# Cross-attention in float32 scores by 32-row bands, weighted sums by 32-column bands, and the clamp on GpSimd

## The chip, the cores and the metric

The kernel runs on one core of a Trainium2 chip. The metric is the device time of one execution in microseconds (us), the median of several runs. One execution works through a batch of 64 sequences.

## The reference, cut to what matters

Two blocks follow each other: a cross-attention with 16 heads of 8 columns over 77 keys (what the change rewrites), and a self-attention with a feed-forward part.

```python
# block 0: x (64,128,128), ctx (64,77,128), mask (64,1,128,77), H = 16, hd = 8
q = (query @ Wq + bq).reshape(B, Qlen, H, hd).transpose(0, 2, 1, 3)
k = (key_in @ Wk + bk)...
v = (key_in @ Wv + bv)...
scores = jnp.einsum('bhqd,bhkd->bhqk', q, k) / jnp.sqrt(jnp.float32(hd))
scores = ALPHA * (scores * mask) + (1.0 - ALPHA) * scores      # ALPHA = 0.5
scores = jnp.clip(scores, -50.0, 50.0)
attn = jax.nn.softmax(scores, axis=-1)
context = jnp.einsum('bhqk,bhkd->bhqd', attn, v)
out = context @ Wo + bo
resid = query + out            # then a layer norm with gamma and beta
# block 1: rms norm, q/k/v of 16 heads of 64, rotary, segments of 64 with 16 persistent and
# 16 (equal) memory keys, softmax, to_out_w, residual, rms norm, gated feed-forward of 341
```

## The kernel before

Each engine has its own program, written by hand, and they meet at semaphores. The work of a sequence is cut into three stages: c (cross-attention), a (self-attention up to the weighted values) and f (output projection and feed-forward). `pipeline` (L322) calls each engine's `body(c, a, f)` so that in a pass of the loop stage c works on sequence i+2, a on i+1 and f on i. The order inside `body` is the order in which an engine meets the stages' parts; nothing reorders them. All the parts of a pass thus stand in one fixed queue per engine. PSUM's eight banks are shared out by `banks` (L50): two for stage c, four for a, two for f. The tasks of a stage take its banks in turn, and `cross_free(task)` waits until the task before in that bank was read.

Keys lie on the partitions of the cross scores, so no maximum is taken: the clamp at 50 bounds the exponent. The 16 heads are four groups g of four heads r, and a group's four score maps fill one bank (77 x 512).

- ACT takes q and k from PSUM (L533 to L545): q0T and k0T in float32, q0T_hi and k0T_hi rounded to float32r, then four masked copies of each (qmask_hi keeps the rows of head r of every group, kmask_hi those of group g). POOL works out the rests of the rounding (L418, L419) and spreads them (`lower`, L411 to L414).
- PE `cross_scores(t)` (L840): three float32r matmuls of 512 columns for group t, hi x hi, hi x lo and lo x hi.
- DVE `masked(t)` (L648) multiplies by the mask's weight wT from PSUM into z0, and `clamped(t)` (L653) clamps z0 in place. Their order is masked 0, 1, clamped 0, 1, masked 2, 3, clamped 2, 3. ACT `exp_cross(t)` (L520) follows each clamp.
- PE `weigh_cross(t)` (L848): 16 heads by the exponentials z0. v0's windows are 64 columns wide, 32 of them the values (zero but for the head's own 8), 32 ones that give the sum of the exponentials. Group 2t goes to PSUM partitions 0 to 63, group 2t+1 to 64 to 127.
- DVE `context_sums(t)` (L660) takes the reciprocal of bank pv t, `context(t)` (L664) multiplies two 32-row pieces each into c0T, PE's L996 multiplies by Wo, and DVE goes on with r (L758) and the layer norm.

The rest of the loop that the prediction speaks of: POOL's `rotated(name)` (L406) adds the two halves of the rotary product for q0, k0, q1 and k1, and PE's `turn(name)` (L858, product at L863) waits for it. hn (L702) is the normalised input of the feed-forward. Between PE's turns stand cross scores 2 and 3 and the projection of v1. Behind the turns comes `weigh_cross`, and behind that the products for the self-attention's maxima (L979, L982), which DVE reduces at L730. mt (L735, L739) are the maxima in two bfloat16 parts, PE's shift (L990) turns them, and scores(2), scores(3) (L872) stand between it and L996. A PE row of the profile is one pass of a matmul; a float32 matmul shows two, a float32r or bfloat16 one shows one.

## Time and profile before

| | |
|---|---|
| time, median of 3 runs | 1803.2 us (1799.8, 1803.2, 1804.67) |
| profiled execution | span 1801.7 us from its first to its last instruction, 52360 instructions; its time outside the span is not listed apart, and the three runs' times lie 1.9 below to 3.0 above the span |
| granted TensorE clock | 0.997 of full speed over the span |
| DMA | 26.14 MB, 15 GB/s in the mean |

A row of the timeline gives the start and the length in us, engine, line, operation, what is written and read (partitions x elements), how many instructions were merged, and in brackets the idle time ahead with what ended it. PE's rows hold the latency of a matmul, so rows that follow each other overlap; the distance of the starts is what each takes in a queue. PEld are PE's weight loads.

### The profile page before, as it was taken

The numbers are of one execution on the slowest core, as the hardware profiler recorded it, in microseconds if no ns is written. First come the engines' busy times: TensorE is split into PE (matmuls) and PEld (weight loads), VectorE is DVE, ScalarE is ACT, GpSimd is POOL, SyncE is SP. The second block draws the span as 40 slices with busy tenths as digits, with TensorE's granted clock in tenths as the row PEclk, the third lists the DMA queues.
The fourth block names the chain that finished last, engine by engine and source line by source line (L and its number), as shares of the span: only waits on it lengthen the run. The fifth ranks groups of instructions, "written<-read, shape, count | busy, mean of one in ns | idle before, by whom it ended". The sixth has DMA issues, their size and how long they took to land.

```text
span 1801.7 us, 52360 instructions
## 1 busy us (share of the span) xinstructions
PE 1666.4 (92%) x17891; PEld 1434.9 (80%) x17891; DVE 1543.8 (86%) x3730; ACT 1073.9 (60%) x2637; POOL 856.9 (48%) x1107
## 2 busy tenths in 40 slices
PE   4899999999999999999999999999999999999997
PEld 3788788788888887888888888887888888878876
DVE  5788888889889889888888888888888898898894
ACT  3555656655656656656556556566566556566563
POOL 4344534535535535445445445445355355355352
PEclk9999999999999999999999999999999999999999
DMA  6000000000000000000000000000000000000000
GB/s 176 17 9 11 10 10 11 8 13 11 8 13 11 8 13 11 8 11 12 8 11 13 8 11 13 8 11 8 12 11 8 13 11 8 13 11 8 13 6 6
DMA packets 32411, 26.14 MB, mean 15 GB/s; under 512 B 8118, under 2 KB 31179, under 8 KB 32139
## 3 DMA queue, kind: packets, MB, share of 16 engines
q1 hardware_dynamic: 32394, 25.93, 5.4%
q8 instruction: 9, 0.15, 0.0%
q14 instruction: 8, 0.06, 0.0%
HBM read 21.46 MB, written 4.46 MB: 14 GB/s over the span
## 4 chain that ended last, share of the span: by engine, by line
DVE 49%; PE 22%; issue 21%; ACT 3%; POOL 3%; DVEq 1%; DMA 1%; SPq 0%; ACTq 0%; POOLq 0%
DVE z L658 9%; PE psum L927 6%; DVE ra L641 5%; DVE z L650 5%; DVE rb L644 5%; DVE mx L730 4%; PE psum L854 4%; DVE rden L662 3%; PE psum L898 3%; DVE sT L752 3%; DVE o L676 3%; DVE c0T L668 2%; ACT z L523 2%; POOL st L464 2%; DVE y L770 1%
## 5 line engine op out<-in xcount | busy, mean ns | idle before, releaser
L409 POOL TENSOR_TENSOR ra<-ra,rb 128x512 f32<-128x512 f32 x256 | 332.2, 1324 | 0.2
L464 POOL TENSOR_TENSOR st<-st,nhalf 128x1 f32<-128x1 f32 x64 | 38.3, 598 | 535.4 <-DVE st L763 535.4
L872 PE MATMUL psum<-qpad,kall 128*81 128x128 f32 x2048 | 251.6, 276 | 0.0
L641 DVE TENSOR_TENSOR ra<-psum,rope 128x512 f32<-128x512 f32 x256 | 174.3, 681 | 77.9 <-PE psum L838 77.8
L872 PEld LDWEIGHTS psum<-qpad,kall 128*81 128x81 f32 x2048 | 224.9, 151 | 2.6
L658 DVE TENSOR_SCALAR z<-z 77x512 f32<-77x512 f32 x256 | 216.8, 885 | 0.0
L581 ACT ACTIVATE probs<-psum 81x512 f32<-81x512 f32 x256 | 131.3, 593 | 142.3 <-PE psum L880 142.3
L523 ACT ACTIVATE z<-z 77x512 f32<-77x512 f32 x256 | 154.1, 627 | 67.1 <-DVE z L658 65.5
L854 PE MATMUL psum<-z,v 77*64 77x128 f32 x2048 | 141.6, 280 | 44.9 <-ACT z L523 44.9
L644 DVE TENSOR_TENSOR rb<-psum,rope 128x512 f32<-128x512 f32 x256 | 173.0, 676 | 0.0
L836 PE MATMUL psum<-wqkv_hi,xnT_hi 128*128 128x512 f32 x384 | 168.6, 439 | 2.7 <-DVE xnT_lo L681 1.8
L854 PEld LDWEIGHTS psum<-z,v 77*64 77x64 f32 x2048 | 112.5, 138 | 69.6 <-issue 68.6
L650 DVE TENSOR_TENSOR z<-psum,wT 77x512 f32<-77x512 f32 x256 | 163.1, 674 | 4.8 <-PE psum L846 4.8
L418 POOL TENSOR_TENSOR q0T_rest<-q0T,q0T_hi 128x128 f32<-128x128 f32 x64 | 29.3, 457 | 288.9 <-ACT k0T_hi L537 288.9
L472 ACT ACTIVATE qpad<-psum 64x512 f32<-64x512 f32 x256 | 151.9, 593 | 3.1
L472 ACT ACTIVATE vall<-psum 64x512 f32<-64x512 f32 x256 | 151.2, 591 | 3.1
L838 PE MATMUL psum<-wqkv_hi,xnT_lo 128*128 128x512 f32 x384 | 152.9, 398 | 0.0
L837 PE MATMUL psum<-wqkv_lo,xnT_hi 128*128 128x512 f32 x384 | 152.4, 397 | 0.0
L863 PE MATMUL psum<-cross_w,ra 128*128 128x128 f32 x1024 | 143.2, 273 | 0.1
L863 PEld LDWEIGHTS psum<-cross_w,ra 128*128 128x128 f32 x1024 | 122.2, 141 | 20.7 <-ACT vall L472 0.4
L888 PE MATMUL psum<-vall,probs 81*64 81x65 f32 x4096 | 133.6, 223 | 0.3 <-ACT probs L581 0.3
L888 PEld LDWEIGHTS psum<-vall,probs 81*64 81x64 f32 x4096 | 124.8, 137 | 8.0 <-issue 0.4
(141 smaller groups left out, 4028.3 us busy)
## 6 DMA issues: line engine op xcount, KB each, us to landing
seq_in<-in SPq DMA_DIRECT2D x64, 166.5 KB
out<-out_sb SPq DMA_DIRECT2D x64, 64.0 KB, 1.6
maskT<-in SPq DMA_DIRECT2D x64, 38.5 KB
vall<-memv_dram SPq DMA_DIRECT2D x128, 4.0 KB, 1.9
ctx_all<-in SPq DMA_DIRECT2D x5, 320.0 KB, 12.3
wqkv<-in SPq DMA_DIRECT2D x1, 1536.0 KB, 10.1
stage<-in SPq DMA_DIRECT2D x1, 1296.0 KB
ctx_all<-in SPq DMA_DIRECT2D x3, 288.0 KB, 11.3
```

The costliest lines, as they stand in the source:

```text
L409: nc.gpsimd.tensor_tensor(ra[:, sl], ra[:, sl], rb[:, sl], ALU.add).then_inc(rot_ready, 1)
L472: copy = lambda out, in_, **k: nc.scalar.activation(out, in_, ACT.Copy, **k)
L523: nc.scalar.activation(zt, zt, ACT.Exp, scale=float(HD0) ** -0.5).then_inc(exp0_ready, 1)
L641: V.tensor_tensor(ra[:, sl].rearrange("n (h d) -> n h d", h=8), p, rope[:, 0, :].unsqueeze(1).broadcast_to([S, 8, DH]), ALU.mult)
L644: V.tensor_tensor(rb[:, sl].rearrange("n (h e t) -> n h e t", h=8, t=2), p, rope[:, 1, :].rearrange("n (e t) -> n e t", t=2).unsqueeze(1). ...
L650: V.tensor_tensor(z0[:, 4 * t:4 * t + 4, :], cross_at(f"score{t}")[0:S2, :].rearrange("k (h q) -> k h q", h=4), wT[:].unsqueeze(1).broadca ...
L658: V.tensor_scalar(zt, zt, lim, -lim, ALU.min, ALU.max).then_inc(clip_ready, 1)
L836: mm(self_at(name), xnT_hi[:], wqkv_hi[:, w], stop=False)
L854: last = mm(cross_at(f"pv{t}")[half:half + 64, 0:S], v0_flat[:, lo:lo + 64], z0[:, 4 * g + r, :], start=r == 0, stop=r == 3)
L863: last = nc.tensor.transpose(self_at(f"{name}T")[:, 128 * n:128 * (n + 1)], ra[:, lo + 128 * n:lo + 128 * (n + 1)], ident[:])
L872: mm(self_at(f"score{t}")[0:KEYS, 128 * n:128 * (n + 1)], kall[:, pair, s, :], qpad[:, pair, s, :, :].rearrange("p h i -> p (h i)"), start ...
L888: last = mm(self_at(f"pv{t}")[SEG * s:SEG * (s + 1), VW * n:VW * (n + 1)], probs[:, pair, s, h, :], vall[s][:, w:w + VW])
```

## The change

ACT writes k0T and q0T once each, in float32. POOL spreads k0T alone: kmask[:, r, :] keeps the rows of head r of all four groups. A group's score is now a float32 matmul over its own band of 32 rows (rows 32g to 32g+31 hold its four heads), one matmul per head of 128 columns, two groups taking turns. v0 has windows of 32 columns, and the sums of the exponentials come from products of their own with a table `ones0`; both write bank "pv", columns 0 to 127 and 128 to 255, group g on partitions 32g to 32g+31. One reciprocal and one product of 128 rows make c0T. The clamps move to POOL, between the rotary sums. Stage c has seven PSUM tasks where it had eight. The tiles of the split operands go.

```diff
+VROW = HD0 * GROUP + HD0
...
-                    pool.wait_ge(qk0_ready, c + 1)
-                    nc.gpsimd.tensor_tensor(q0T_rest[:], q0T[:], q0T_hi[:].bitcast(F32), ALU.subtract)
-                    nc.gpsimd.tensor_tensor(k0T_rest[:], k0T[:], k0T_hi[:].bitcast(F32), ALU.subtract).then_inc(rest0_step, 1)
-                    pool.wait_ge(rest0_step, c + 1)
-                    lower(1)
+                def clamped(t):
+                    lim = CLAMP * float(HD0) ** 0.5
+                    zt = z0[:, 4 * t:4 * t + 4, :]
+                    pool.wait_ge(z_ready, c * 4 + (t + 1))
+                    passed(pool, pool_passed)
+                    nc.gpsimd.tensor_scalar(zt, zt, lim, -lim, ALU.min, ALU.max).then_inc(clip_ready, 1)
+
+                if c is not None:
+                    pool.wait_ge(k0_ready, c + 1)
+                    nc.gpsimd.tensor_tensor(kmask[:], headmask.unsqueeze(2).broadcast_to([D, GROUP, S2]),
+                                            k0T[:].unsqueeze(1).broadcast_to([D, GROUP, S2]), ALU.mult).then_inc(kmask_ready, 1)
...
-                if c is not None:
-                    lower(0).then_inc(lo0_ready, 1)
...
-                    for name in QK:
-                        rotated(name)
+                    rotated("q0")
+                    rotated("k0")
+                if c is not None:
+                    clamped(0)
+                    clamped(1)
+                if a is not None:
+                    rotated("q1")
+                    rotated("k1")
+                if c is not None:
+                    clamped(2)
+                    clamped(3)
...
-                    for dst in (q0T, q0T_hi):
-                        nc.scalar.activation(dst[:], p[:, 0:S], ACT.Identity, bias=cols[:, BQ:BQ + 1])
-                    for dst in (k0T, k0T_hi):
-                        last = nc.scalar.activation(dst[:], p[:, S:S + S2], ACT.Identity, bias=cols[:, BK:BK + 1])
-                    last.then_inc(qk0_ready, 1)
-                    for r in range(GROUP):
-                        nc.scalar.activation(qmask_hi[:, r, :], p[:, 0:S], ACT.Identity,
-                                             scale=headmask[:, 0, r:r + 1], bias=head_bias[:, 0, r:r + 1])
-                    for g in range(GROUP):
-                        nc.scalar.activation(kmask_hi[:, g, :], p[:, S:S + S2], ACT.Identity,
-                                             scale=headmask[:, 1, g:g + 1], bias=head_bias[:, 1, g:g + 1])
+                    wait(act, (kmask_ready, c))
+                    nc.scalar.activation(k0T[:], p[:, S:S + S2], ACT.Identity, bias=cols[:, BK:BK + 1]).then_inc(k0_ready, 1)
+                    nc.scalar.activation(q0T[:], p[:, 0:S], ACT.Identity, bias=cols[:, BQ:BQ + 1])
...
-                def context_sums(t):
-                    wait(dve, cross_filled(f"pv{t}", c))
-                    V.reciprocal(rden0[:, t, :], cross_at(f"pv{t}")[:, 0:S]).then_inc(cross_step, 1)
+                def context_sums():
+                    wait(dve, cross_filled("pv", c))
+                    V.reciprocal(rden0[:], cross_at("pv")[:, S:2 * S]).then_inc(cross_step, 1)
+
+                def context():
+                    wait(dve, (cross_step, cross_steps[1]("rden0", c)))
+                    V.tensor_tensor(c0T[:], cross_at("pv")[:, 0:S], rden0[:], ALU.mult).then_inc(c0T_ready, 1)
...
-                    masked(0)
-                    masked(1)
-                    clamped(0)
-                    clamped(1)
-                    masked(2)
-                    masked(3)
-                    clamped(2)
-                    clamped(3)
+                    for t in range(4):
+                        masked(t)
...
-                def cross_scores(t):
-                    wait(pe, cross_free(f"score{t}", c))
-                    out = cross_at(f"score{t}")[0:S2, :]
-                    q_hi, q_lo = (m[:].rearrange("p r i -> p (r i)") for m in (qmask_hi, qmask_lo))
-                    mm(out, kmask_hi[:, t, :], q_hi, stop=False)
-                    mm(out, kmask_hi[:, t, :], q_lo, start=False, stop=False)
-                    mm(out, kmask_lo[:, t, :], q_hi, start=False).then_inc(cross_fill(f"score{t}"), 1)
+                def cross_scores(*groups):
+                    for g in groups:
+                        wait(pe, cross_free(f"score{g}", c))
+                    for r in range(GROUP):
+                        for g in groups:
+                            rows = slice(32 * g, 32 * (g + 1))
+                            last = mm(cross_at(f"score{g}")[0:S2, S * r:S * (r + 1)], kmask[rows, r, :], q0T[rows, :], start=r == 0)
+                            if r == GROUP - 1:
+                                last.then_inc(cross_fill(f"score{g}"), 1)
+
+                def weigh_cross(*groups):
+                    for r in range(GROUP):
+                        window = slice(32 * r, 32 * (r + 1))
+                        for g in groups:
+                            mm(cross_at("pv")[32 * g:32 * (g + 1), 0:S], v0[:, g, window], z0[:, 4 * g + r, :], start=r == 0)
+                        for g in groups:
+                            last = mm(cross_at("pv")[32 * g:32 * (g + 1), S:2 * S], ones0[:, window], z0[:, 4 * g + r, :], start=False)
+                    return last
...
+                    wait(pe, cross_free("pv", c))
+                    pe.wait_ge(exp0_ready, c * 4 + 2)
+                    weigh_cross(0, 1)
+                    pe.wait_ge(exp0_ready, c * 4 + 4)
+                    weigh_cross(2, 3).then_inc(cross_fill("pv"), 1)
```

How the queues move. On POOL, in the loop, the stretch from the pow of the feed-forward's norm (st) to the copy of memk; `ra` is the rotary sum, `z` the clamp. Before:

```order
L424 TENSOR_TENSOR st<-st,nhalf 128x1
L413 TENSOR_TENSOR qmask_lo<-cross_w,q0T_rest 128x512
L407 ISA
L409 TENSOR_TENSOR ra<-ra,rb 128x512
L407 REGISTER_ALU
L409 TENSOR_TENSOR ra<-ra,rb 128x512
L407 REGISTER_ALU
L409 TENSOR_TENSOR ra<-ra,rb 128x512
L407 REGISTER_ALU
L409 TENSOR_TENSOR ra<-ra,rb 128x512
```

And now:

```order
L420 TENSOR_TENSOR st<-st,nhalf 128x1
L403 ISA
L405 TENSOR_TENSOR ra<-ra,rb 128x512
L403 REGISTER_ALU
L405 TENSOR_TENSOR ra<-ra,rb 128x512
L410 ISA
L412 TENSOR_SCALAR z<-z 77x512
L410 REGISTER_ALU
L412 TENSOR_SCALAR z<-z 77x512
L403 REGISTER_ALU
L405 TENSOR_TENSOR ra<-ra,rb 128x512
```

Two clamps stand ahead of q1's and k1's rotary sums, and two more behind k1's.

On DVE, in the loop, from the last rotary product (rb of k1) to the first copy of kall. Before:

```order
L644 TENSOR_TENSOR rb<-psum,rope 128x512
L709 REGISTER_ALU
L99 ISA
L650 TENSOR_TENSOR z<-psum,wT 77x512
L99 REGISTER_ALU
L650 TENSOR_TENSOR z<-psum,wT 77x512
L658 TENSOR_SCALAR z<-z 77x512 x2
L650 TENSOR_TENSOR z<-psum,wT 77x512
L99 REGISTER_ALU
L650 TENSOR_TENSOR z<-psum,wT 77x512
L658 TENSOR_SCALAR z<-z 77x512
```

And now:

```order
L638 TENSOR_TENSOR rb<-psum,rope 128x512
L692 REGISTER_ALU
L100 ISA
L644 TENSOR_TENSOR z<-psum,wT 77x512
L100 ISA
L644 TENSOR_TENSOR z<-psum,wT 77x512
L100 REGISTER_ALU
L644 TENSOR_TENSOR z<-psum,wT 77x512
L100 REGISTER_ALU
L644 TENSOR_TENSOR z<-psum,wT 77x512
L100 ISA
L700 COPY kall<-psum 128x8x64
```

The four masks stand together, each behind a wait of its own.

On PE, in the loop, from the last turn (k1) to the first product for the maxima; `z` and `v` are the weighted sums. Before:

```order
L863 MATMUL psum<-cross_w,ra 128x128 x4
L99 REGISTER_ALU
L854 MATMUL psum<-z,v 64x128 x8
L99 REGISTER_ALU
L854 MATMUL psum<-z,v 64x128 x8
L972 REGISTER_ALU
L979 MATMUL psum<-causal_b,ident_b 128x4x64
```

And now, where the first four rows of sums come four times for groups 0 and 1 and as often for groups 2 and 3:

```order
L836 MATMUL psum<-cross_w,ra 128x128 x4
L100 REGISTER_ALU
L826 MATMUL psum<-z,v 32x128 x2
L828 MATMUL psum<-z,ones 32x128 x2
L826 MATMUL psum<-z,v 32x128 x2
L828 MATMUL psum<-z,ones 32x128 x2
```

16 matmuls of 64 weight columns have become 32 of 32 columns, in the same place.

## Rows read from the trace of the kernel before

**Rows 1.** The page, busy time of each engine, and the chain by engine

```profile
PE 1666.4 (92%) x17891; PEld 1434.9 (80%) x17891; DVE 1543.8 (86%) x3730; ACT 1073.9 (60%) x2637; POOL 856.9 (48%) x1107
...
DVE 49%; PE 22%; issue 21%; ACT 3%; POOL 3%; DVEq 1%; DMA 1%; SPq 0%; ACTq 0%; POOLq 0%
```

**Rows 2.** The chain in order of time: start us, us, what

```profile
917.72 0.32 PE psum L905
...
944.97 0.32 PE psum L905
```

**Rows 3.** Timeline of DVE, 923.4 to 941.5

```profile
924.04 0.60 DVE L702 TENSOR_SCALAR hn<-x,st 128x128 f32<-128x128 f32 x1
...
926.96 1.27 DVE L650 TENSOR_TENSOR z<-psum,wT 77x512 f32<-77x512 f32 x2
928.15 1.85 DVE L658 TENSOR_SCALAR z<-z 77x512 f32<-77x512 f32 x2
929.93 1.27 DVE L650 TENSOR_TENSOR z<-psum,wT 77x512 f32<-77x512 f32 x2
931.13 1.56 DVE L658 TENSOR_SCALAR z<-z 77x512 f32<-77x512 f32 x2
...
935.11 1.72 DVE L730 TENSOR_REDUCE mx<-psum 128x4 f32<-128x324 f32 x4 [0.36 <-PE psum L982]
...
938.62 1.19 DVE L668 TENSOR_TENSOR c0T<-psum,rden 32x128 f32<-32x128 f32 x4
...
940.63 0.28 DVE L758 TENSOR_TENSOR r<-psum,xb 128x128 f32<-128x128 f32 x1
```

**Rows 4.** Timeline of POOL, 923.4 to 934.9

```profile
923.00 0.55 POOL L424 TENSOR_TENSOR st<-st,nhalf 128x1 f32<-128x1 f32 x1 [0.23 <-DVE st L692]
923.52 1.03 POOL L413 TENSOR_TENSOR qmask_lo<-cross_w,q0T_rest 128x512 fp32r<-128x512 f32 x1
924.52 5.20 POOL L409 TENSOR_TENSOR ra<-ra,rb 128x512 f32<-128x512 f32 x4
...
932.97 0.29 POOL L457 TENSOR_SCALAR y_keep<-y 128x128 f32<-128x128 f32 x1
```

**Rows 5.** Timeline of PE, 924 to 941.5

```profile
925.01 0.42 PE L844 MATMUL psum<-qmask_hi,kmask_hi 128*77 128x512 f32 x1
...
931.17 0.60 PE L863 MATMUL psum<-cross_w,ra 128*128 128x128 f32 x4
931.70 1.09 PE L854 MATMUL psum<-z,v 77*64 77x128 f32 x16
933.49 1.09 PE L854 MATMUL psum<-z,v 77*64 77x128 f32 x16 [0.69 <-ACT z L523]
934.62 0.28 PE L979 MATMUL psum<-causal_b,ident_b 128*128 128x256 bf16 x1
...
938.00 0.22 PE L990 MATMUL psum<-stack_b,mt 128*64 128x64 bf16 x1
938.15 1.97 PE L872 MATMUL psum<-qpad,kall 128*81 128x128 f32 x16
939.96 0.39 PE L996 MATMUL psum<-cross_w,c0T 128*128 128x128 f32 x2
```

**Rows 6.** Timeline of ACT, 929 to 936

```profile
932.72 0.63 ACT L523 ACTIVATE z<-z 77x512 f32<-77x512 f32 x1 [0.52 <-DVE z L658]
```

**Rows 7.** Timeline of DVE in the first sequence, 21 to 31, POOL idle

```profile
24.76 0.75 DVE L658 TENSOR_SCALAR z<-z 77x512 f32<-77x512 f32 x2
```

**Rows 8.** Groups by line of POOL, 0 to 60: busy us, mean ns | idle

```profile
L452 POOL TENSOR_TENSOR wqkv_lo<-wqkv,wqkv_hi 128x3072 fp32r<-128x3072 f32 x1 | 6.7, 6695 | 4.1 <-ACT wqkv_hi L472 4.1
```

**Rows 9.** Timelines of PE, first sequence and 915; a group of weight loads

```profile
24.38 1.98 PE L854 MATMUL psum<-z,v 77*64 77x128 f32 x16 [0.26 <-ACT z L523]
...
915.05 2.09 PE L888 MATMUL psum<-vall,probs 81*64 81x65 f32 x64
...
L872 PEld LDWEIGHTS psum<-qpad,kall 128*81 128x81 f32 x2048 | 224.9, 151 | 2.6
```

More of the change, by code:

```diff
@@ L158, in build @@
         k0T = sb("k0T", [D, S2])
-        q0T_hi, k0T_hi = sb("q0T_hi", [D, S], F32R), sb("k0T_hi", [D, S2], F32R)
-        q0T_rest, k0T_rest = sb("q0T_rest", [D, S]), sb("k0T_rest", [D, S2])
-        qmask_hi, qmask_lo = (sb(n, [D, GROUP, S], F32R) for n in ("qmask_hi", "qmask_lo"))
-        kmask_hi, kmask_lo = (sb(n, [D, GROUP, S2], F32R) for n in ("kmask_hi", "kmask_lo"))
-        VB = 4 * HD0 + 40
-        v0 = sb("v0", [S2, 4, 4, VB])
+        kmask = sb("kmask", [D, GROUP, S2])
+        v0 = sb("v0", [S2, GROUP, GROUP * VROW])
+        ones0 = sb("ones0", [S2, GROUP * VROW])
         z0 = sb("z0", [S2, H, S])
-        rden0 = sb("rden0", [128, 2, S])
+        rden0 = sb("rden0", [128, S])
         c0T = sb("c0T", [D, S])
@@ L596, in _ @@
             dve.wait_ge(cross_w_in, CROSS_WEIGHTS_IN)
-            for which, bias in ((0, BQ), (1, BK)):
-                V.tensor_scalar(head_bias[:, which, :], headmask[:, which, :], cols[:, bias:bias + 1], None, ALU.mult)
             dve.wait_ge(setup_pe, 1)
@@ L651, in masked @@
                                     wT[:].unsqueeze(1).broadcast_to([S2, 4, S]), ALU.mult).then_inc(z_ready, 1)
-                def clamped(t):
-                    lim = CLAMP * float(HD0) ** 0.5
-                    zt = z0[:, 4 * t:4 * t + 4, :]
-                    dve.wait_ge(z_ready, c * 4 + (t + 1))
-                    passed(dve, dve_passed)
-                    V.tensor_scalar(zt, zt, lim, -lim, ALU.min, ALU.max).then_inc(clip_ready, 1)
-                def context_sums(t):
-                    wait(dve, cross_filled(f"pv{t}", c))
-                    V.reciprocal(rden0[:, t, :], cross_at(f"pv{t}")[:, 0:S]).then_inc(cross_step, 1)
-                def context(t):
-                    wait(dve, (cross_step, cross_steps[1](f"rden{t}", c)))
-                    for half in (0, 64):
-                        row = 64 * t + half // 2
-                        last = V.tensor_tensor(c0T[row:row + 32, :], cross_at(f"pv{t}")[half:half + 32, 0:S],
-                                               rden0[half + 32:half + 64, t, :], ALU.mult)
-                    last.then_inc(c0T_ready, 1)
+                def context_sums():
[4 more added lines that the diff above has]
+                    V.tensor_tensor(c0T[:], cross_at("pv")[:, 0:S], rden0[:], ALU.mult).then_inc(c0T_ready, 1)
                 def normalised(t):
@@ L724, in body @@
                                       self_at(f"k{t}T").rearrange("p (c s j) -> p c s j", c=4, s=NSEG)).then_inc(k_ready, 1)
-                if c is not None:
-                    context_sums(0)
                 if a is not None:
@@ L742, in body @@
                 if c is not None:
-                    context_sums(1)
-                if c is not None:
-                    context(0)
-                    context(1)
+                    context_sums()
+                    context()
                 if f is not None:
@@ L838, in project @@
                     mm(self_at(name), xnT_lo[:], wqkv_hi[:, w], start=False).then_inc(self_fill(name), 1)
-                def cross_scores(t):
-                    wait(pe, cross_free(f"score{t}", c))
-                    out = cross_at(f"score{t}")[0:S2, :]
-                    q_hi, q_lo = (m[:].rearrange("p r i -> p (r i)") for m in (qmask_hi, qmask_lo))
-                    mm(out, kmask_hi[:, t, :], q_hi, stop=False)
-                    mm(out, kmask_hi[:, t, :], q_lo, start=False, stop=False)
-                    mm(out, kmask_lo[:, t, :], q_hi, start=False).then_inc(cross_fill(f"score{t}"), 1)
-                def weigh_cross(t):
-                    wait(pe, cross_free(f"pv{t}", c))
-                    pe.wait_ge(exp0_ready, c * 4 + (2 * t + 2))
-                    for r in range(4):
-                        for g in (2 * t, 2 * t + 1):
-                            half, lo = 64 * (g % 2), 4 * VB * g + 64 * r
-                            last = mm(cross_at(f"pv{t}")[half:half + 64, 0:S], v0_flat[:, lo:lo + 64],
-                                      z0[:, 4 * g + r, :], start=r == 0, stop=r == 3)
-                    last.then_inc(cross_fill(f"pv{t}"), 1)
+                def cross_scores(*groups):
[15 more added lines that the diff above has]
+                    return last
                 def turn(name):
@@ L941, in body @@
                     pe.wait_ge(qkv0_ready, c + 1)
-                    pe.wait_ge(lo0_ready, c + 1)
-                    cross_scores(0)
-                    cross_scores(1)
+                    pe.wait_ge(kmask_ready, c + 1)
+                    cross_scores(0, 1)
                 if f is not None:
```

39 lines of the change are left out of this document (15 added, 24 removed).

## The prediction

> **What bounds the kernel now.** The page comes first [rows 1]: DVE is busy 86% of the span, PE 92% (modelled ends), POOL 48%, and the chain that ended last runs 49% on DVE and 22% on PE. So the loop is a ring of hand-overs and not one full engine. The chain in order of time shows the ring's length: xnT's transpose (L905) starts at 917.72 and again at 944.97 [rows 2], 27.25 us for one sequence. All times below are of this one pass. DVE's timeline [rows 3] shows the work around the change: the masks z (L650) from 926.96, two at a time, the clamps (L658), the maxima (L730) from 935.11, four small c0T products (L668), r (L758) at 940.63. PE's timeline [rows 5] gives what those wait for: scores 0 (L844) from 925.01, the last turn of k1 (L863) at 931.17, weighted sums (L854) at 931.70 and 933.49, the first maxima product (L979) at 934.62, shift (L990) at 938.00, the last scores (L872) up to L996 (wo) at 939.96. POOL [rows 4] adds ra and rb four times, 5.20 us, 1.30 each, from 924.52 to 929.72, ahead of need.
>
> **The change part by part.**
>
> *ACT* loses ten activations and writes k0T first; it waits for others in this stretch, so I cost that at nothing. Its cover is PE's three projections before L844. POOL's kmask product replaces four products, the last of which (L413) ends at 924.55 [rows 4]. POOL then starts its first ra+rb right behind the pow (L424), at 923.55 and not at 924.52.
>
> *hn.* hn (L702) took 0.60 us and ended at 924.64, 0.09 after POOL's L413 ended at 924.55 [rows 3, 4]: it stood behind a POOL operation. The first ra+rb now covers it and ends at 924.85, so hn ends near 924.94: DVE +0.30. The masks then start at 927.26.
>
> *Clamps, price on POOL.* No POOL clamp is in the trace. DVE's took 0.75 us for two with POOL idle [rows 7], 1.85 and 1.56 beside POOL [rows 3]; 0.37 each is my lower end. The nearest POOL row is y_keep's tensor_scalar with two constants, 128 columns in 0.29 [rows 4]. A POOL operation with two inputs costs 1.30 for 512 columns and 6.70 for 3072 [rows 4, 8], 2.1 ns a column and some 0.2 fixed. With the same 0.2 fixed, y_keep's 0.29 leaves 0.7 to 0.9 ns a column, so 512 columns cost 0.2 + 0.45 = 0.65. I take 0.65, since that row is the same operation. Upper ends: 1.03, the product with a repeated input (L413), and 1.30.
> The Trainium skill ("GPSIMD Engine Reference", section Key points) speaks against the move: for elementwise work DVE is about twice as fast. No POOL clamp here can confirm it. An estimate by it is 0.75 for a clamp (twice 0.37), and the forecast at the end would be about 1890.
>
> *Clamps, place on POOL.* The order is q0, k0, clamp 0, clamp 1, q1, k1, clamp 2, clamp 3. k0 ends at 924.9 + 1.3 = 926.2. Mask 0 ends near 927.95 (0.635 a mask, two in 1.27 [rows 3]), so POOL now stands idle from 926.2 to 928.0 with q1 and k1 queued behind that wait. Then clamps 0 and 1 to 929.3, q1 and k1 to 931.9 (were 929.72), clamps 2 and 3 to 933.2, exp 3 (0.63 [rows 6]) to 933.9.
>
> *DVE.* 3.41 us of clamps leave it (1.85 + 1.56), but this does not bring the later masks forward: masks 2 and 3 need scores that PE starts only when masks 0 and 1 have emptied both banks (928.55), so they run near 929.95, as before. DVE idles instead.
>
> *Scores on PE.* Twelve records with 512 moving columns become 32 with 128. A float32 record of this length with full rows takes 0.109 (16 in 1.97, less the 0.27 tail), and 0.054 where two column halves take turns (16 in 1.09) [rows 5]. Two 32-row bands take turns here, which no row shows. Ends: 0.054 and 0.109, 0.9 or 1.75 us for two groups. I take 0.054. It costs nothing either way: the first two groups start at 925.3 (925.01 plus hn's 0.3), and at 0.109 they are full at 925.3 + 1.75 + 0.27 = 927.3, as DVE comes free for them (927.26), and masks 2 and 3 end at 932.65, before POOL is at clamp 3.
>
> *Weighted sums on PE.* 32 records become 64, since the sums of weights are products of their own. Each call has 32 records over two column bands: at 0.054 that is 1.74 per call where 0.9 stood. L888 gets 0.03 a record, but with 65 moving columns [rows 9]: per column it is the same rate, so fewer weight columns should buy nothing. Upper end 0.109, if bands of 32 did not run side by side.
>
> *Sum up to the maxima.* k1 turned: 931.9 + 0.1, 0.45 of issue, to 932.45. Groups 0 and 1 from 932.5 to 934.25, groups 2 and 3 (exp 3 is done at 933.9) to 936.0. L979 starts at 936.05 instead of 934.62: **+1.43**.
>
> *After the maxima.* DVE: one reciprocal is left; the first stood in an idle gap before the maxima, worth nothing. c0T falls from 1.19 to about 0.29 (one product of 128 rows, as r's [rows 3]): -0.9. PE: shift at 938.00 + 1.43 = 939.43, eight scores behind it, wo at 939.96 + 1.43 = 941.39. PE was just in step with c0T; now it is the later one, so most of the 0.9 is lost. wo is full 0.44 later (as 939.96 to 940.40) at 941.83, and r, at 940.63 before, starts there: **+1.20** per sequence. From r to the next L905 DVE works as before (ending at 944.97), and its sums (L888) come 1.43 later on PE, just in time.
>
> *Total.* 63 passes hold both parts: 63 x 1.20 = 76. The first sequence has nothing to hide its longer sums, and the clock is at its lower level there (16 records in 1.98 [rows 9] against 1.09): about +2. The profiled span is 1801.7, the median 1.5 above: 1801.7 + 76 + 2 + 1.5 = **1881**.
>
> **Bounds.** Clamp 0.37: clamp 1 ends 928.9, k1 931.5, L979 935.6, +0.75 a pass: 1852. Clamp 1.03: k1 ends 932.7, clamp 3 934.7, exp 3 935.4, L979 937.25, +2.4: 1956. At 1.30: L979 938.3, 2025.
>
> **Rivals.**
> *A, faster.* DVE's relief decides. For it: 49% of the chain is DVE, and the clamps cost double beside POOL. It needs a clamp of 0.37 and sums at 0.027 a record. Then k1 ends at 931.5, L979 starts at 934.0, 0.62 earlier, and with a wo no longer late (-0.23) a pass is 0.85 shorter: 1801.7 - 54 + 2 + 1.5 = 1751. It turns where L979 starts before 934.85. Against it: the columns' rate of L854 and L888, and POOL's idle wait. 6%.
> *B, slower by the row bands.* Their weight loads (0.15 each, L872 on PEld [rows 9]) are not hidden. At 0.109 + 0.15 a record scores 0 and 1 fill only at 929.7, scores 2 and 3 at 936.1, and L979 starts near 940.5: +5.6, 2160. From about 0.12 on it begins to cost; half-way (0.17) L979 is at 937.95, +3.1 a pass, 2000. Against it: L854's loads hide in the same kind of turn. 7%.
> *C, clamp as a two-input operation,* 1.03 to 1.30: 1956 to 2025. Against it: y_keep. 6%.
> *D, no relief and no harm:* the 0.3 of hn does not come and the waits pack tighter than my 0.1 a hand-over, with a clamp of 0.37: within 0.3%, up to 1809. 3%.
> *E, the bands of 32 columns do not overlap:* 3.5 us per call, L979 at 939.5, +4.7 a pass: 2101. 2%.
>
> **Numbers.** Forecast 1881, its cases from 1835 (the 0.37 clamp and 0.25 us fewer in hand-overs) to 1956: 76%. A measurement of this kernel tells 0.3% (5 us) from nothing. Faster 6%, same 3%, slower 91% (forecast, B, C and E). The range 1835 to 1970 holds the forecast's cases and the near end of C, the larger part of its 6%; A, B, D, E and the rest, 2 in 10, lie outside.
>
> **What would show it.** After: L905 to L905 near 28.45; POOL's clamps 0.6 to 0.7 each, with idle time of some 1.8 before clamp 0, released by DVE's mask; DVE busy share down to about 65%; 32 sum records in about 2.0 us; L979 right behind the last sum with no wait for exp 3; r waiting for L996. It is wrong if q1 and k1 end before 931, if a clamp is above 0.8 (then exp 3 releases the last sums), if score records are above 0.12, or if DVE still has no idle time ahead of masks 2 and 3.

## The result, and the profile after

| | before | after |
|---|---|---|
| time, median (lowest to highest) | 1801.85 us (1799.80 to 1804.67) | 1820.99 us (1819.94 to 1823.03) |
| span of the profiled execution | 1801.7 us | 1821.2 us |
| one pass (xnT's transpose to the next) | 27.25 us | 27.53 us |
| granted TensorE clock | 0.997 | 0.996 |

The ratio is 1.0102, with a 95% interval of 1.0087 to 1.0118. The change makes the kernel slower, by 19 us where the prediction said 78 and put its lower end at 1835.

First the page of the changed kernel: busy time of each engine, the chain by engine, and two groups (line, engine, operation; busy us, mean ns; idle time ahead and who ended it).

```profile
PE 1707.5 (94%) x21219; PEld 1511.1 (83%) x21219; DVE 1232.4 (68%) x3216; ACT 874.1 (48%) x1997; POOL 840.0 (46%) x1172
...
PE 38%; issue 31%; DVE 16%; POOL 13%; POOLq 1%; DMA 1%; DVEq 0%; SPq 0%; ACT 0%; ACTq 0%
...
L705 DVE TENSOR_REDUCE mx<-psum 128x4 f32<-128x324 f32 x256 | 109.0, 487 | 183.7 <-PE psum L956 183.7
L412 POOL TENSOR_SCALAR z<-z 77x512 f32<-77x512 f32 x256 | 153.3, 614 | 148.5 <-DVE z L644 148.5
```

Against [rows 1], DVE went from 86% to 68% busy and from 49% to 16% of the chain, and the time still rose. POOL, 3% of the chain before, now holds 13%, and waits 148.5 us for masks. DVE waits 183.7 us for the maxima products. The relief of DVE turned into waiting.

POOL's timeline of one pass, which begins at 927.42 (start, length, line; the bracket is the idle time ahead and its end):

```profile
932.47 0.55 POOL L420 TENSOR_TENSOR st<-st,nhalf 128x1 f32<-128x1 f32 x1 [1.58 <-DVE st L675]
932.99 2.52 POOL L405 TENSOR_TENSOR ra<-ra,rb 128x512 f32<-128x512 f32 x2
937.55 1.20 POOL L412 TENSOR_SCALAR z<-z 77x512 f32<-77x512 f32 x2 [2.05 <-DVE z L644]
938.72 2.52 POOL L405 TENSOR_TENSOR ra<-ra,rb 128x512 f32<-128x512 f32 x2
```

A clamp takes 0.60 on POOL. Ahead of clamp 0 POOL is idle for 2.05 us with q1 and k1 queued behind it; k1 is added at 941.24, 13.82 us into the pass, where it was 12.0 before (929.72 in [rows 4]).

PE's timeline of the same pass:

```profile
934.84 1.10 PE L818 MATMUL psum<-q0T,kmask 32*77 32x128 f32 x16
...
940.13 0.63 PE L836 MATMUL psum<-cross_w,ra 128*128 128x128 f32 x4 [0.77 <-POOL ra L405]
...
941.94 0.41 PE L826 MATMUL psum<-z,v 77*32 77x128 f32 x4
942.18 0.39 PE L828 MATMUL psum<-z,ones 77*32 77x128 f32 x4
...
943.27 0.43 PE L826 MATMUL psum<-z,v 77*32 77x128 f32 x8
943.49 0.43 PE L828 MATMUL psum<-z,ones 77*32 77x128 f32 x8
943.75 0.39 PE L826 MATMUL psum<-z,v 77*32 77x128 f32 x4
...
945.16 0.28 PE L953 MATMUL psum<-causal_b,ident_b 128*128 128x256 bf16 x1
...
950.19 0.39 PE L970 MATMUL psum<-cross_w,c0T 128*128 128x128 f32 x2
```

L953 is the old L979, L970 the old L996. PE now waits 0.77 for the first turn that follows the clamps. The 64 records of the sums take 3.22 us from 941.94 to 945.16. Four records take 0.22; but at 943.27 and 943.49, where the first call (groups 0 and 1) meets the second (2 and 3), eight records pass in 0.22 and the next eight in 0.26.

DVE's timeline of the same pass:

```profile
932.09 0.29 DVE L675 CUSTOM_DVE_ANT_0 x1sq<-x 128x128 f32<-128x128 f32 x1
...
933.67 0.70 DVE L685 TENSOR_SCALAR hn<-x,st 128x128 f32<-128x128 f32 x1
...
936.68 1.27 DVE L644 TENSOR_TENSOR z<-psum,wT 77x512 f32<-77x512 f32 x2
939.40 1.28 DVE L644 TENSOR_TENSOR z<-psum,wT 77x512 f32<-77x512 f32 x2 [1.44 <-PE psum L818]
...
945.64 1.70 DVE L705 TENSOR_REDUCE mx<-psum 128x4 f32<-128x324 f32 x4 [2.90 <-PE psum L956]
...
949.14 0.29 DVE L653 TENSOR_TENSOR c0T<-psum,rden 128x128 f32<-128x128 f32 x1
...
950.62 0.29 DVE L731 TENSOR_TENSOR r<-psum,xb 128x128 f32<-128x128 f32 x1 [0.41 <-PE psum L970]
```

The idle time stands where the prediction put it: 1.44 ahead of masks 2 and 3, and r waits 0.41 for wo.

The same stretch as positions in the pass, worked out from these rows and those of before:

| us into the pass | before | predicted | after |
|---|---|---|---|
| masks start | 9.24 | 9.54 | 9.26 |
| k1 added on POOL | 12.00 | 14.18 | 13.82 |
| first weighted sum | 13.98 | 14.78 | 14.52 |
| first maxima product | 16.90 | 18.33 | 17.74 |
| wo (L996, L970) | 22.24 | 23.67 | 22.77 |
| r | 22.91 | 24.11 | 23.20 |

The spans differ by 19.5, and it adds up like this. The first xnT product starts at 35.31 in both kernels. The second starts at 73.64 where it was 70.64: 3.0 in one sequence. There too POOL meets clamp 0 ahead of q1 and k1, and waits 9.45 us for its mask (the first row below): k1's rotary sum ends at 58.52 where it ended at 48.00, and the weighted sums start 2.13 later, at 60.58 against 58.45. The clock was lower for a part of it. The third is at 101.19 (97.88), the last at 1780.88 (1762.33): 18.55 less 3.31 is 15.2 over 61 passes, 0.25 each, since seven passes before were longer than 27.25 (27.52 to 28.48). The end after the last adds 0.95. After the change, a row of POOL's timeline, two of PE's, and the windows row of 58 to 62 (PE, PEld, DVE, ACT, POOL busy, then the granted clock):

```profile
54.85 1.21 POOL L412 TENSOR_SCALAR z<-z 77x512 f32<-77x512 f32 x2 [9.45 <-DVE z L644]
```

```profile
35.31 0.45 PE L878 MATMUL psum<-cross_w,xn 128*128 128x128 f32 x1 [3.74 <-DVE xn L758]
73.64 0.33 PE L878 MATMUL psum<-cross_w,xn 128*128 128x128 f32 x1 [0.65 <-DVE o L659]
```

```profile
58.00:62.00 4.00, 4.00 (x34) 3.24 (x34) 1.32 (x3) 2.81 (x5) 2.49 (x6) 0.64 0.17 35
```

### The profile page after: what moved, and what is told of

Same layout as the page of the kernel before. It is cut to its first block, busy times and chain, and to the rows that moved or that the text cites. A ratio compares the mean times of both kernels' runs of the same rounds, so it can differ in the third digit from the quotient of the medians.

```text
span 1821.2 us, 57993 instructions
## 1 busy us (share of the span) xinstructions
PE 1707.5 (94%) x21219; PEld 1511.1 (83%) x21219; DVE 1232.4 (68%) x3216; ACT 874.1 (48%) x1997; POOL 840.0 (46%) x1172
## 4 chain that ended last, share of the span: by engine, by line
PE 38%; issue 31%; DVE 16%; POOL 13%; POOLq 1%; DMA 1%; DVEq 0%; SPq 0%; ACT 0%; ACTq 0%
PE psum L845 13%; PE psum L826 6%; PE psum L828 5%; POOL ra L405 5%; DVE rb L638 4%; DVE ra L635 4%; PE psum L836 4%; POOL kmask L416 2%; DVE z L644 2%; PE psum L956 2%; POOL st L467 2%; POOL z L412 2%; POOL st L420 2%; PE psum L953 2%; DVE bn L733 1%
## 5 line engine op out<-in xcount | busy, mean ns | idle before, releaser
L405 POOL TENSOR_TENSOR ra<-ra,rb 128x512 f32<-128x512 f32 x256 | 322.2, 1280 | 0.1
L845 PE MATMUL psum<-qpad,kall 128*81 128x128 f32 x2048 | 251.8, 276 | 0.0
L705 DVE TENSOR_REDUCE mx<-psum 128x4 f32<-128x324 f32 x256 | 109.0, 487 | 183.7 <-PE psum L956 183.7
L845 PEld LDWEIGHTS psum<-qpad,kall 128*81 128x81 f32 x2048 | 225.0, 151 | 2.7
L412 POOL TENSOR_SCALAR z<-z 77x512 f32<-77x512 f32 x256 | 153.3, 614 | 148.5 <-DVE z L644 148.5
L836 PE MATMUL psum<-cross_w,ra 128*128 128x128 f32 x1024 | 147.6, 277 | 48.9 <-POOL ra L405 48.3
L836 PEld LDWEIGHTS psum<-cross_w,ra 128*128 128x128 f32 x1024 | 112.3, 141 | 82.5 <-issue 81.4
L826 PE MATMUL psum<-z,v 77*32 77x128 f32 x2048 | 179.7, 278 | 0.7 <-DVE z L644 0.7
L828 PE MATMUL psum<-z,ones 77*32 77x128 f32 x2048 | 178.0, 275 | 0.0
L416 POOL TENSOR_TENSOR kmask<-cross_w,k0T 128x308 f32<-128x308 f32 x64 | 45.2, 707 | 242.7 <-ACT k0T L538 242.7
L475 ACT ACTIVATE hnT<-psum,cols 128x128 f32<-128x128 f32 x64 | 23.6, 368 | 277.7 <-PE psum L912 277.7
L818 PE MATMUL psum<-q0T,kmask 32*77 32x128 f32 x2048 | 142.7, 277 | 11.7 <-DVE z L644 8.8
```

Source lines behind the costliest of these rows:

```text
L405: nc.gpsimd.tensor_tensor(ra[:, sl], ra[:, sl], rb[:, sl], ALU.add).then_inc(rot_ready, 1)
L412: nc.gpsimd.tensor_scalar(zt, zt, lim, -lim, ALU.min, ALU.max).then_inc(clip_ready, 1)
L475: copy = lambda out, in_, **k: nc.scalar.activation(out, in_, ACT.Copy, **k)
L826: mm(cross_at("pv")[32 * g:32 * (g + 1), 0:S], v0[:, g, window], z0[:, 4 * g + r, :], start=r == 0)
L828: last = mm(cross_at("pv")[32 * g:32 * (g + 1), S:2 * S], ones0[:, window], z0[:, 4 * g + r, :], start=False)
L836: last = nc.tensor.transpose(self_at(f"{name}T")[:, 128 * n:128 * (n + 1)], ra[:, lo + 128 * n:lo + 128 * (n + 1)], ident[:])
```

## The experiments

The theory: the loss comes from where the clamps stand in POOL's queue and from the longer sums, and neither a cheaper DVE nor the new scores cost anything. The rivals: the move to GpSimd itself is what hurts, or the new scores are; or the bands of 32 columns do not share the array. Each run is named by its change against the kernel before or after, and a ratio is to the kernel before as it was run beside it, with its 95% interval. The probes e3, e6 and e8 stand below with their times.

| run | scores | sums | clamps | time us | ratio |
|---|---|---|---|---|---|
| before | old | old | DVE | 1801.9 | 1 |
| after | new | new | POOL, between | 1821.0 | 1.010 |
| e1 | new | new | POOL, behind | 1764.5 | 0.980 (0.977 to 0.984) |
| e2 | new | new | DVE | 1763.7 | 0.979 (0.976 to 0.981) |
| e4 | new | new, one call | POOL, between | 1810.0 | 1.004 (1.003 to 1.006) |
| e5 | old | old | POOL, between | 1801.1 | 1.000 (0.999 to 1.001) |
| e7 | new | old | POOL, between | 1802.6 | 1.001 (0.999 to 1.002) |
| e9 | new | new, one call | POOL, behind | 1758.2 | 0.976 (0.974 to 0.977) |
| e10 | new | new, one call | DVE | 1771.9 | 0.982 (0.980 to 0.984) |
| e11 | new | old | DVE | 1753.6 | 0.974 (0.972 to 0.976) |
| e12 | new | old | POOL, behind | 1745.8 | 0.968 (0.967 to 0.969) |

### e1_late_clamps: the clamps behind all four rotary sums

```diff
-                    rotated("q0")
-                    rotated("k0")
+                    for name in QK:
+                        rotated(name)
                 if c is not None:
-                    clamped(0)
-                    clamped(1)
-                if a is not None:
-                    rotated("q1")
-                    rotated("k1")
-                if c is not None:
-                    clamped(2)
-                    clamped(3)
+                    for t in range(4):
+                        clamped(t)
```

> The changed kernel with POOL's order q0, k0, q1, k1, then clamps 0 to 3. Theory 1 (POOL's queue order is the costly part: q1 and k1 stand behind a wait for DVE's mask, 2.05 us idle per pass in the changed trace): k1's rotary sum ends about 3 us earlier, the sums start behind k1's turn near 13.4 us into a pass instead of 14.5, L953 starts near 16.7 instead of 17.7, and the pass falls by 0.9 to 1.0: about 1760 (1745 to 1775), faster than both kernels. Theory 2 (PE's longer sums alone make the kernel slower, what POOL does is hidden): within 4 us of 1821.

Measured 1764.54 us (1763.37 to 1771.19), ratio 0.9803. POOL's timeline of this run, one pass, and then the chain by engine:

```profile
903.77 3.91 POOL L405 TENSOR_TENSOR ra<-ra,rb 128x512 f32<-128x512 f32 x3
907.65 1.18 POOL L412 TENSOR_SCALAR z<-z 77x512 f32<-77x512 f32 x2
909.84 1.21 POOL L412 TENSOR_SCALAR z<-z 77x512 f32<-77x512 f32 x2 [1.00 <-DVE z L638]
```

```profile
PE 80%; DVE 10%; issue 5%; POOL 3%; DMA 1%; DVEq 0%; ACT 0%; SPq 0%; ACTq 0%; POOLq 0%
```

The 2.05 us of idle time ahead of clamp 0 are gone, and the idle time that is left, ahead of clamp 2, holds up no rotary sum. The move of the clamps behind the rotary sums is worth 56 us, and the chain now runs 80% on PE. The place in the queue is the cause, not the engine.

### e2_dve_clamps: the clamps back on DVE, in the old order

```diff
-                    for t in range(4):
-                        masked(t)
+                    masked(0)
+                    masked(1)
+                    clamped(0)
+                    clamped(1)
+                    masked(2)
+                    masked(3)
+                    clamped(2)
+                    clamped(3)
```

> The changed kernel with the clamps back on DVE in the old order (masks 0, 1, clamps 0, 1, masks 2, 3, clamps 2, 3), bands and sums as changed. Theory 1: k1 is turned early again, but exp 3 comes as late as before the change (about 15.9 us into a pass), so groups 2 and 3 of the sums end near 17.5, and the time lies between the two kernels, 1810 (1802 to 1818). Rival (the clamp on POOL is in itself what costs, since it is slower there than a free DVE): below 1795.

Measured 1763.71 us (1762.89 to 1764.33): 46 us below the expectation. By its number this is the rival's result (below 1795), but not by its cause: e1 leaves the clamps on POOL and takes 1764.5. Two clamps on DVE took 0.91 and 1.00 here, where [rows 3] has 1.85 and 1.56. DVE's timeline, then POOL's:

```profile
907.72 0.91 DVE L636 TENSOR_SCALAR z<-z 77x512 f32<-77x512 f32 x2
...
910.48 1.00 DVE L636 TENSOR_SCALAR z<-z 77x512 f32<-77x512 f32 x2
```

```profile
902.83 5.16 POOL L405 TENSOR_TENSOR ra<-ra,rb 128x512 f32<-128x512 f32 x4
907.94 0.41 POOL L426 COPY kall<-memk 128x16 f32 x1
...
910.53 0.67 POOL L436 TENSOR_TENSOR xb<-seq_in,rows 128x128 f32<-128x128 f32 x1
```

POOL's timeline of before, beside clamps 2 and 3:

```profile
931.11 1.29 POOL L445 TENSOR_TENSOR ug<-ug,half_gate 128x384 f32<-128x384 f32 x1
```

Without the split operands POOL starts its rotary sums earlier and ends them at 907.99, 0.27 us into the first two clamps. In the kernel before, clamps 0 and 1 lay almost wholly beside the rotary sums (928.15 to 930.00 against an end at 929.72) and took 1.85. In all four cases the second clamp of a pair ends 0.28 or 0.29 behind the end of a POOL operation beside it: 930.00 behind 929.72 and 932.69 behind 932.40 before, 908.63 behind 908.35 and 911.48 behind 911.20 here. That the price follows the POOL operation beside it is my reading of these rows; no run moved the overlap alone.

### e3_no_weight_sums: the sums of the exponentials left out

```diff
-                        for g in groups:
-                            last = mm(cross_at("pv")[32 * g:32 * (g + 1), S:2 * S], ones0[:, window], z0[:, 4 * g + r, :], start=False)
```

> The changed kernel without the products with ones0, so without the sums of the exponentials: it divides by the weighted values instead, and its output is not the attention's. 64 records fall to 32. Theory 1: L953 then starts behind exp 3, near 16.65 us into a pass (was 17.74), ACT's value copy holds the fourth maxima product again as before the change, and the time is 1788 (1780 to 1796), 33 below the changed kernel. If PE's sums were hidden: within 4 us of 1821.

Measured 1787.10 us (1785.71 to 1792.27). The reciprocal is taken of the weighted values instead, so the result is no attention; the work is otherwise the same. PE's timeline, the fourth maxima product:

```profile
926.41 0.28 PE L951 MATMUL psum<-causal_b,ident_b 128*128 128x256 bf16 x1 [0.24 <-ACT vall L475]
```

Half the records gone give 34 us, and a wait caps it: with the sums early, the fourth maxima product waits for ACT's copy of values(1) (vall). This wait is a step that the prediction did not have.

### e4_four_bands: all four groups in one call behind exp 3

```diff
-                    pe.wait_ge(exp0_ready, c * 4 + 2)
-                    weigh_cross(0, 1)
...
-                    weigh_cross(2, 3).then_inc(cross_fill("pv"), 1)
+                    weigh_cross(0, 1, 2, 3).then_inc(cross_fill("pv"), 1)
```

> The changed kernel with all four groups taking turns in one call of the weighted sums, which then waits for exp 3 (15.6 us into a pass, the sums began at 14.5). If bands of 32 columns run side by side however many they are (at the joint of the two calls 16 records passed in 0.48 us, where four took 0.22 each time elsewhere): 0.027 us a record, the sums end near 17.5, 1803 (1795 to 1812). If only two can: 0.055 a record, they end near 19.2, 1910 (1890 to 1925).

Measured 1809.98 us (1808.93 to 1814.83): 11 us faster than after, 7 above the expected 1803 and within its 1795 to 1812. PE's timeline:

```profile
912.30 0.42 PE L826 MATMUL psum<-z,v 77*32 77x128 f32 x8 [1.10 <-ACT z L526]
912.54 0.40 PE L828 MATMUL psum<-z,ones 77*32 77x128 f32 x8
912.76 0.40 PE L826 MATMUL psum<-z,v 77*32 77x128 f32 x8
...
914.18 0.28 PE L951 MATMUL psum<-causal_b,ident_b 128*128 128x256 bf16 x1
```

Eight records per 0.22 us throughout: four bands of 32 columns run side by side, 0.027 a record where two bands give 0.055. The 64 records take 1.88 instead of 3.22. This confirms what the joint of the two calls showed.

### e5_before_pool_clamps: the kernel before, with only the clamps moved

The edit is that of the change's own diff for `clamped`, in the kernel before.

> The kernel before with only the clamps moved: POOL's order q0, k0, clamps 0 and 1, q1, k1, clamps 2 and 3, masks 0 to 3 in a row on DVE; operands, scores and sums stay. By the schedule: clamps of 0.60, k1's rotary sum ends 13.8 us into a pass instead of 12.0, exp 3 at 15.7 as before, ACT's value copy still holds the fourth maxima product (18.1), so the move alone costs nothing: 1802 (1794 to 1808). Rival (the clamps' place costs the 40 us by which the two variants of the changed kernel with other places were faster): above 1820.

Measured 1801.06 us (1799.84 to 1807.20), ratio 1.0000. In the kernel before, the move buys and costs nothing. Its fourth maxima product shows the wait again:

```profile
932.63 0.28 PE L982 MATMUL psum<-causal_b,ident_b 128*128 128x256 bf16 x1 [0.23 <-ACT vall L488]
```

### e6_before_sums_twice: the kernel before, half of its sums run twice

```diff
-                    for r in range(4):
+                    for r in (*range(4 * t), *range(4)):
```

> The kernel before with the weighted sums of groups 2 and 3 run twice (the second run starts the accumulation again, so the output is the same): L979 comes about 0.87 us later, as late in a pass (17.75) as in the changed kernel. If the old tail on DVE (maxima, mt, reciprocal, four c0T products, sT, r, end to end) has no slack, a pass grows by nearly all of it: 1850 (1842 to 1858). If such a delay is absorbed there as in the changed kernel (0.28 of 0.84): 1820.

Measured 1849.72 us (1846.93 to 1852.47). Sixteen more records (0.87 us) cost 0.75 a pass. So in the kernel before almost nothing catches longer sums, since r stands there at the end of DVE's serial part: what longer sums cost in the changed kernel depends on its shorter DVE part.

### e7_old_sums and e8_four_products: what the new sums cost and give

e7 puts the old sums into the changed kernel (windows of 64 columns, 32 records, two banks, two reciprocals, four products). e8 keeps the new sums, but makes c0T by four products of 32 rows:

```diff
-                    V.tensor_tensor(c0T[:], cross_at("pv")[:, 0:S], rden0[:], ALU.mult).then_inc(c0T_ready, 1)
+                    for row in range(0, 128, 32):
+                        last = V.tensor_tensor(c0T[row:row + 32, :], cross_at("pv")[row:row + 32, 0:S],
+                                               rden0[row:row + 32, :], ALU.mult)
+                    last.then_inc(c0T_ready, 1)
```

> The changed kernel with the old weighted sums (64-column windows with their ones, 32 records, two banks, two reciprocals, four c0T products); clamps on POOL, bands for the scores. L953 starts behind exp 3 at 16.65 us into a pass, ACT's value copy holds the fourth product, DVE's tail is as before: as the kernel before, 1803 (1796 to 1810). If the longer sums were not what moved the time (POOL's queue alone): within 4 us of 1821.

> The changed kernel with c0T by four products of 32 rows (1.2 us on DVE where one took 0.29). In its trace c0T was ready 0.76 before PE came to L970 and r waited 0.41 for L970. So of the 0.9 more 0.45 should show per pass: 1849 (1842 to 1857), which is the size of what the one product had given. If PE alone sets r: 1821.

Measured: e7 1802.64 us (1800.87 to 1807.88), e8 1856.76 (1853.17 to 1858.50). The new sums cost 18 us as they stand, and without the shorter c0T they would cost 54. e7 differs from e5 by the scores alone, 1802.6 against 1801.1: as long as POOL's queue holds the clamps between the rotary sums, the new scores are worth nothing.

### e9_late_four, e10_dve_four, e11_dve_old_sums: combinations

e9 is e1 with e4's single call, e10 is e2 with it, and e11 is e2 with e7's old sums, so that of the change only the scores are left.

> The changed kernel with both orders altered: POOL adds q0, k0, q1, k1 before the four clamps, and the weighted sums of all four groups run in one call behind exp 3, each record over its own band of 32 columns. With the late clamps alone exp 3 ended at 911.71 and the maxima products followed the last sum at about 913.8. In one call 64 records took 1.76 us (912.30 to 914.06 in the run with four bands alone), so here 911.75 to 913.5: up to 0.3 us a pass earlier, until the fourth maxima product waits for ACT's copy of values(1), which ends at 914.16 there. My theory: PE is now the bound and waits stand behind it, 1752 to 1764, likeliest 1758. Rival, that the sums of groups 0 and 1 filled an idle stretch ahead of exp 3 which now stays empty: 1768 or more.

> The changed kernel with the clamps back on DVE in the old order, and the sums of all four groups in one call behind exp 3. With the clamps on DVE alone exp 3 ended at 912.14 and the sums ran from 910.90 to 914.1; here 912.2 to 913.96, some 0.12 to 0.15 earlier: 1750 to 1763, likeliest 1756. Rival: the exps, now the last to be waited for, move with DVE beside POOL, and the sums start later than 912.5: 1770 or more.

> The changed kernel with the clamps back on DVE and the old sums with windows of 64 columns (32 records, two banks, two reciprocals, four products): of the change only the float32 scores in 32-row bands are left. The sums end about 1 us earlier than with 64 records, but the fourth maxima product then waits for ACT's copy of values(1) (which ended at 914.59 with the clamps alone), and DVE has the serial tail of four products again, with r at about 919.6, as in the run with the clamps alone. My theory: 1757 to 1770, likeliest 1764, so that the new scores alone give all of the gain. Rival: the serial tail of DVE costs again what it cost before (0.9 us a pass), 1790 or more.

e9: 1758.22 us (1754.36 to 1759.97), at its expected 1758. e11: 1753.55 us (1751.33 to 1759.35), 10 us below the likeliest 1764 and below the range. Its steady pass is 26.47 against 26.66 in e2: the serial tail on DVE gives r at 22.13 into the pass, where I had taken e2's 22.32. The tail of four products is longer than e2's (5.52 from the maxima to r against 4.97), but the maxima start 0.74 earlier, 16.61 into the pass against 17.35.

e10: 1771.88 us (1766.85 to 1779.61), above its range and above the rival's 1770, but not for the rival's reason alone. Its steady pass is 26.61, 0.05 shorter than e2's, which would give a span of about 1759; the profiled one is 1777.7. Here the clock decides. Busy time of the engines by stretch (PE, PEld, DVE, ACT, POOL, then the granted clock), and PE's timeline there:

```profile
221.00:222.50 1.50, 1.33 (x48) 1.33 (x52) 0.66 (x2) 1.44 (x4) 0.04 (x1) 1.00 0.49 140
222.50:224.00 1.50, 1.50 (x35) 1.22 (x28) 0.31 (x1) 1.05 (x2) 0.00 (x0) 0.73 0.00 0
224.00:225.50 1.50, 1.50 (x16) 1.37 (x14) 1.50 (x4) 0.00 (x0) 0.00 (x0) 0.50 0.00 0
225.50:227.00 1.50, 1.50 (x11) 1.50 (x10) 1.37 (x6) 0.00 (x0) 0.00 (x0) 0.63 0.00 0
```

```profile
221.17 0.43 PE L823 MATMUL psum<-z,v 77*32 77x128 f32 x8 [1.23 <-ACT z L510]
...
227.61 0.22 PE L959 MATMUL psum<-stack_b,mt 128*64 128x64 bf16 x1
...
921.76 0.43 PE L823 MATMUL psum<-z,v 77*32 77x128 f32 x8 [1.24 <-ACT z L510]
```

After 1.23 us idle and 1.9 us of sums the granted clock fell to 0.50, the level of 1.2 GHz, for some 3.4 us, and came back while PE was busy throughout. From the first maxima product (223.06) to the shift this pass took 4.55 us; another pass of the same run took 3.10 (923.65 to 926.75), although PE had been idle as long ahead of its sums, 1.24 us. Twelve passes of this trace took 28.04 to 28.09 instead of 26.61, 17.4 us together. e9 has the same call behind an idle stretch of 1.11 us, and its trace shows a clock of 1.00 from 200 to 1700. The kernel before has one such stretch, from 142 to 146, in a pass of 28.48. Why the clock falls in one pass and not in the next, these runs don't tell.

### e12_late_old_sums: the fastest

The changed kernel with e1's order of POOL and e7's old sums.

> The changed kernel with the clamps on GpSimd but behind all four rotary sums (q0, k0, q1, k1, then clamps 0 to 3), and the old sums with windows of 64 columns, two reciprocals and four products. Compared with the run that has the clamps on DVE and the old sums (1753.6, a pass of 26.47): there the second half of the sums waited 0.30 for exp 3 and the fourth maxima product 0.22 for ACT's copy of values(1), which stands behind exp 3 on ACT. Into a pass, exp 3 ends 0.19 earlier with the late clamps on GpSimd (14.77 against 14.96) and that copy about 0.13 earlier (17.22 against 17.35); the serial tail on DVE is the same. My theory: 0.05 to 0.13 a pass, so 1745 to 1751, likeliest 1748. Rival: the tail on DVE binds and not ACT's copy, so that nothing is gained: 1753 to 1757.

Measured 1745.80 us (1743.74 to 1746.00), ratio 0.9681 (0.9668 to 0.9694). PE's timeline, one pass:

```profile
886.05 0.33 PE L881 MATMUL psum<-cross_w,xn 128*128 128x128 f32 x1 [0.58 <-DVE o L656]
...
903.29 0.28 PE L953 MATMUL psum<-causal_b,ident_b 128*128 128x256 bf16 x1 [0.23 <-ACT vall L469]
...
912.40 0.32 PE L881 MATMUL psum<-cross_w,xn 128*128 128x128 f32 x1 [0.57 <-DVE o L656]
```

A pass of 26.35, 0.12 less than in e11: the copy of values(1) releases the fourth product 17.24 into the pass, where 17.22 was expected. The gain is the expected one, but the copy did not set the pace. The chain of this pass, in order of time, runs past it (start us, us, what):

```profile
899.54 0.61 POOL z L412
900.17 0.64 ACT z L520
...
900.95 1.09 PE psum L830 x16
...
903.37 0.91 DVE mx L704 x2
```

From the maxima on it follows DVE's serial tail up to r, 5.52 us here and in e11. So the rival was right that this tail is what ends last. It starts 0.10 earlier than in e11 (16.51 into the pass against 16.61), because exp 3 releases the last sums 0.10 earlier (14.90 against 15.00).

## Why the prediction was half right

**Right: the direction, and its mechanism.** POOL stood idle 2.05 ahead of clamp 0 (said: some 1.8), its clamps took 0.60 (0.65), q1 and k1 came late, the sums ran on into the first maxima product (old L979) without a wait for exp 3, and r waited for wo. Masks 2 and 3 came only 0.23 earlier in the pass (11.98 against 12.21), though 3.41 us of clamps had left DVE. The scores cost nothing and their weight loads were hidden (16 records in 1.03 from their start to the next product), which ends rival B; the clamp price ends C; e4 ends E; the time itself, 1821, ends A and D. e1 shows the place in POOL's queue to be the largest term: 56 us.

**Wrong: the size, 0.28 in the pass followed instead of 1.20.** Three steps of the sum for a pass were mis-sized, and a small one outside it.

*"hn", masks at 927.26: 0.28 of the miss.* The step asked what newly lies beside hn, and hn did take 0.70. It did not ask what no longer lies beside the operation ahead of it. In the kernel before, x1sq ran beside POOL; DVE's timeline of before:

```profile
922.40 0.51 DVE L692 CUSTOM_DVE_ANT_0 x1sq<-x 128x128 f32<-128x128 f32 x1
```

After, it took 0.29. So the pow behind it starts 5.05 into the pass where it started at 5.28, and POOL's first rotary sum at 5.57 where the prediction had 5.83. hn ends 0.12 behind the end of that sum, as predicted (0.09), but this is 6.95 into the pass against 6.92 before. Hand-overs were 0.02 longer from there on, which leaves 0.26 of the miss at the first weighted sum.

*"Weighted sums on PE": 0.33.* "Per column it is the same rate, so fewer weight columns should buy nothing" was read from two bands (L854, L888), where the number of bands was the same. The rate goes by the number of bands side by side: at the joint of the two calls four were in flight. Within each call the 0.054 held. (The sign "32 sum records in about 2.0 us" did not fit the prediction's own 1.74; they took about 1.6.) Together these two make the first maxima product +0.84 instead of +1.43.

*"After the maxima", shift at 938.00 + 1.43: 0.31.* The sum moved all that stands behind L979 by the same amount. But the fourth maxima product was waiting for ACT already, on PE's timeline of before:

```profile
935.84 0.29 PE L979 MATMUL psum<-causal_b,ident_b 128*128 128x256 bf16 x1 [0.23 <-ACT vall L472]
```

ACT's vall ends 18.07 into the pass before and 18.09 after, so this wait was slack for PE. In the changed kernel the row has no wait, and the scores behind it (L872, L845) start only 0.43 later in the pass. The shift behind them starts 0.56 later: by the rows it now follows DVE's mt, which is ready 0.82 later (the shift starts 0.15 behind it, and started 0.41 behind it before, when PE's scores held it); wo is 0.53 later. So of the +0.84 this stretch swallowed 0.31, and r's own slack 0.24 (predicted 0.23): 0.29 is left at r, 0.28 in the pass. e3, e5, e7, e11 and e12 show the wait for ACT back as soon as the sums end earlier. e6 does not contradict this: there r hangs on DVE's long tail, which has no such slack.

*"Total", +2 in the first sequence.* The first sequence lost nothing: its longer sums begin earlier (23.19 where 24.38 stood, [rows 9]), and xnT waits for DVE's xn in both kernels. The second sequence lost 3.0 instead: POOL stood idle for 9.45 us ahead of clamp 0 with q1 and k1 queued behind it, and the clock was granted at 0.64 from 58 to 62. With the clamps behind (e1) this sequence took 36.02 from product to product, against 38.33 after the change and 35.33 before it.

The range failed with them: its bounds moved the clamp's price alone, and held every wait behind L979 to be zero. The three errors all pointed the same way. That the time came out slower at all was no luck, but it was narrow: the same change with the clamps elsewhere (e1, e2) is faster than the kernel before by 2%.

**The rule on GpSimd.** A clamp takes 0.60 on POOL and 0.37 on DVE with POOL idle [rows 7]: 1.6 times. The page "GPSIMD Engine Reference" (Key points) of the Trainium skill has DVE about twice as fast; the measurement decides, and against the 0.45 to 0.50 that a clamp takes on DVE in e2 the distance is smaller still. As a reason against the move it does not hold here: with the clamps behind the rotary sums and the old sums, POOL is the better place by 8 us (e12 against e11), and with the new sums the two places are equal (1764.5 in e1, 1763.7 in e2).

**What the change's parts are worth, alone.** The new scores: 48 us (before against e11, which differ in nothing else), and nothing where POOL's queue is held up (e5 against e7). By the rows the gain comes over DVE's clamps: POOL's rotary sums end 1.3 us earlier in the pass, the two pairs of clamps take 0.90 and 1.00 where they took 1.85 and 1.56, and exp 3 releases the last sums 15.00 into the pass instead of 15.77; the pass is 0.78 shorter. The new sums: a loss of 18 us (after against e7, e1 against e12) or 10 (e2 against e11); run in one call it is 7 (e4 against e7) or 12 (e9 against e12). The clamps between the rotary sums instead of behind them: a loss of 56 (after against e1), 57 (e7 against e12) or 52 (e4 against e9), always with the new scores; no run has the old scores with the clamps behind.

## What to carry to other kernels

On an in-order queue, ask of each moved step what it waits for and what stands behind it: two operations of 0.6 us cost nearly 0.9 us a pass only by standing ahead of work that was ready. When a delay is carried down a chain, subtract every wait for another engine that it passes, also those of 0.2 us; a trace shows them in brackets. Then ask which engine's own chain binds next, since it caps what such a wait can absorb. When work is taken off an engine, look for what its neighbours do in the time that it no longer shares, and not only for what newly collides.
